# Gated cross-attention and a gated expert layer on one core: root refinements, normalised tiles and small constants moved to GpSimd, output accumulators begun from turned x_mid, new orders

## What is computed

```python
x = x + tanh(g_xattn[0]) * xattn(ctx_768, layernorm(x), mask, ...)
#   xn = layernorm(ctx)*g+b; ln = layernorm(latents)*g+b       (latents = layernorm(x))
#   q = ln @ Wq.T;  k, v = split(concat([xn @ Wkv.T, ln @ Wlkv.T]))
#   attn = softmax(where(mask, rmsnorm(q)*SCALE @ rmsnorm(k).T, -max));  out = attn @ v @ Wo.T + bo
x = x + tanh(g_ffn[0]) * ffn(layernorm(x), expert_sel, keys, values)
#   gates = sigmoid(x @ expert_sel.T); the best 4 of 32 are kept, the others are 0
#   out = (relu(x @ keys) * gate) @ values                     (32 experts of 64)
```

## Time and profile before

| | us |
|---|---|
| median of 3 runs | 115.79 (115.44 to 116.35) |
| the profiled execution | 115.75 |
| its span, first to last instruction | 114.0 |
| TensorE busy | 105.8 (93%) |
| VectorE busy | 95.0 (83%) |
| ScalarE busy | 65.6 (58%) |
| GpSimd busy | 16.0 (14%) |

### The profile page before, as it was taken

How to read it: one execution, slowest core, us unless ns; L and a number is a source line. 1 busy time by engine, 2 the same in 40 slices (tenths; PEclk the granted TensorE clock), 3 DMA queues, 4 the chain that set the end, 5 groups by cost and what they waited for, 6 DMA issues and landing times.

```text
span 114.0 us, 2086 instructions
## 1 busy us (share of the span) xinstructions
PE 105.8 (93%) x644; PEld 86.1 (76%) x644; DVE 95.0 (83%) x309; ACT 65.6 (58%) x148; POOL 16.0 (14%) x26
## 2 busy tenths in 40 slices
PE   4993998999999999999989999999999999999980
PEld 4983987868668597959879766678888888888860
DVE  5776688968789699688597999997999999889982
ACT  4918999999879958084611322470666455444410
POOL 6021000002100869140000400000420000000000
PEclk9999999999999999999999999999999999999999
DMA  3789800000000000000001987586008987532004
GB/s 86 223 179 397 376 10 3 3 6 0 0 0 0 6 0 0 0 3 6 0 12 49 297 270 255 178 255 198 3 12 285 299 244 229 214 126 83 0 30 154
DMA packets 7112, 12.78 MB, mean 112 GB/s; under 512 B 894, under 2 KB 2558, under 8 KB 6847
## 3 DMA queue, kind: packets, MB, share of 16 engines
q1 hardware_dynamic: 7102, 12.67, 34.3%
HBM read 12.00 MB, written 0.66 MB: 111 GB/s over the span
## 4 chain that ended last, share of the span: by engine, by line
PE 74%; ACT 12%; DMA 4%; DVE 3%; SPq 3%; issue 1%; DVEq 1%
PE bank L724 13%; PE bank L726 13%; PE bank L725 13%; PE bank L862 10%; PE bank L849 5%; DMA bo<-wb_in 4%; PE bank L916 3%; PE bank L754 3%; PE bank L783 3%; PE bank L794 2%; PE bank L820 2%; PE bank L847 2%; ACT cx L594 1%; ACT kT L657 1%; PE bank L887 1%
## 5 line engine op out<-in xcount | busy, mean ns | idle before, releaser
L701 ACT ACTIVATE hid_hi<-keys 128x512 fp32r<-128x512 f32 x28 | 17.4, 632 | 16.8 <-DVE keys L535 13.1
L535 DVE SCALAR_TENSOR_TENSOR keys<-bank,inT 128x512 f32<-128x512 f32 x32 | 21.2, 686 | 1.1 <-PE bank L726 0.8
L552 DVE TENSOR_TENSOR hid_lo<-keys,hid_hi 128x512 fp32r<-128x512 f32 x28 | 18.4, 686 | 0.1
L862 PE MATMUL bank<-vw,prob 128*128 128x129 f32 x128 | 15.7, 278 | 0.2 <-ACT prob L670 0.2
L862 PEld LDWEIGHTS bank<-vw,prob 128*128 128x128 f32 x128 | 14.8, 191 | 1.0 <-issue 1.0
L724 PE MATMUL bank<-xm_hi,k_lo 128*128 128x512 f32 x32 | 13.7, 427 | 0.0
L726 PE MATMUL bank<-xm_hi,k_hi 128*128 128x512 f32 x32 | 12.5, 391 | 0.0
L725 PE MATMUL bank<-xm_lo,k_hi 128*128 128x512 f32 x32 | 12.5, 390 | 0.0
L445 DVE CUSTOM_DVE_ANT_0 junk<-bank,mask_b 128x512 bf16<-128x512 f32 x16 | 10.4, 689 | 2.0 <-PE bank L820 1.8
L724 PE MATMUL bank<-hid_hi,v_lo 128*128 128x512 f32 x28 | 11.3, 402 | 0.0
L670 ACT ACTIVATE prob<-bank 128x512 f32<-128x512 f32 x16 | 8.7, 594 | 4.0 <-PE bank L849 3.8
(11 more groups left out here) (131 smaller groups left out, 198.8 us busy)
## 6 DMA issues: line engine op xcount, KB each, us to landing
inT<-gate_rows SPq DMA_DIRECT2D x32, 256.0 KB, 3.6
keys<-keys_in SPq DMA_DIRECT2D x1, 1024.0 KB, 7.5
values<-values_in SPq DMA_DIRECT2D x1, 1024.0 KB, 9.5
out<-x_mid SPq DMA_DIRECT2D x4, 128.0 KB, 1.8
vecs_x<-x_in SPq DMA_DIRECT2D x1, 256.0 KB, 5.0
wa<-wa_in SPq DMA_DIRECT2D x1, 208.0 KB, 2.9
cx<-ctx_in SPq DMA_DIRECT2D x2, 96.0 KB, 2.6
cx<-ctx_in SPq DMA_DIRECT2D x1, 192.0 KB, 5.5
```

Source lines behind the costliest of these rows:

```text
L535: dve.scalar_tensor_tensor(hid[:, n % 3, :], bank[H_BANK[n % len(H_BANK)]][:, :], 0.0, gated[:, n % SLOTS, :], ALU.max, ALU.mult).then_inc ...
L552: dve.tensor_tensor(hid_lo[:, m % RING, :], hid[:, n % 3, :], hid_hi[:, m % RING, :].bitcast(F32), ALU.subtract).then_inc(hid_lo_ready, 1)
L701: act.activation(hid_hi[:, m % RING, :], hid[:, n % 3, :], ACT.Copy).then_inc(hid_hi_ready, 1)
L862: last = pe.matmul(bank_of(b, OUT + t)[:, WOA * a:WOA * a + WOA], prob[:, b % 2, a, j, P * t:P * t + P], vw[:, b, j, a, :], start=(j == 0) ...
```

## The change

GpSimd gets an order of its own and takes over stages:

- `norm_in` (root refinement, nb, the x tiles), `newton_qk` (the refinement of `norm_qk`; VectorE's `norm_qk` then waits for `rs_qk_ready`), `norm_mid` whole, the rounded parts of expert_sel (`split_sel`), 1 + exp for the sigmoid (`add_one`) and the scaling of bo (`scale_bo`, before at the end of ScalarE's `constants`). The refinement is four instructions there, each waiting for the one before. GpSimd's wait for `max_done` ahead of the low parts is gone, and each quarter is a stage.
- `turn_res` writes x_mid transposed into the accumulator bank as its first contents; every `down` adds to it. The gates are scaled by tanh(g_ffn) when they are copied out, and `finish` is a plain copy: for the first half on ScalarE, for the second on VectorE. `x_midT` and ScalarE's copy of it are gone.
- The orders of TensorE, VectorE and ScalarE are new.

```diff
 PE_ORDER = """
...
+    warm 13, warm 14, turn_in 0, warm 15, warm 16, warm 17, warm 18, fold 0, project 0, turn_in 1, vlat 0,
+    vctx 0, warm 19, project 1, vlat 1, warm 20, turn_qk 0, turn_in 2, warm 21, vctx 1, warm 22, warm 23,
+    row_max 0.0, vlat 2, vctx 2, row_max 0.1, turn_in 3, turn_qk 1, project 2, turn_max 0, vlat 3, row_max 1.0,
+    weights 0.0, vctx 3, row_max 1.1, weights 0.1, project 3, turn_max 1, turn_qk 2, attend 0.0, weights 1.0,
+    row_max 2.0, turn_qk 3, weights 1.1, row_max 2.1, row_max 3.0, attend 0.1, turn_max 2, attend 1.0,
+    row_max 3.1, attend 1.1, weights 2.0, turn_max 3, turn_mid 0, weights 2.1, weights 3.0, select 0, turn_mid 1,
+    attend 2.0, select 1, weights 3.1, turn_gates 0, attend 2.1, turn_gates 1, attend 3.0, attend 3.1,
+    turn_res 0, turn_mid 2, up 0.0, up 0.1, select 2, up 0.2, turn_res 1, up 0.3, up 0.4, down 0.0, down 0.1,
+    turn_mid 3, down 0.2, up 0.5, down 0.3, up 0.6, up 0.7, up 0.8, down 0.4, up 0.9, up 0.10, down 0.5,
+    down 0.6, select 3, turn_gates 2, up 0.11, down 0.7, down 0.8, up 0.12, turn_gates 3, up 0.13, up 0.14,
+    turn_res 2, down 0.9, turn_res 3, down 0.10, up 0.15, up 1.0, down 0.11, down 0.12, up 1.1, down 0.13,
...
+POOL_ORDER = """
+    norm_in 0, norm_in 1, scale_bo 0, add_bias 0, newton_qk 0, norm_in 2, mask 0, norm_in 3, newton_qk 1,
+    low_values 0, newton_qk 2, newton_qk 3, low_values 1, low_keys 0, low_keys 1, add_bias 1, low_keys 2,
+    norm_mid 0, split_sel 0, low_values 2, norm_mid 1, low_keys 3, add_one 0, add_one 1, norm_mid 2,
+    low_values 3, norm_mid 3, add_one 2, add_one 3
 """
 DVE_ORDER = """
...
+    stats_in 0, stats_in 1, scale_wo 0, stats_in 2, sum_qk 0, stats_in 3, norm_qk 0, scale_gq 0, sum_qk 1,
+    row_max 0.0, norm_qk 1, row_max 0.1, turn_max 0, row_max 1.0, sum_qk 2, row_max 1.1, norm_qk 2, sum_qk 3,
+    turn_max 1, norm_qk 3, row_max 2.0, row_max 2.1, row_max 3.0, out_proj 0, turn_max 2, stats_mid 0,
+    row_max 3.1, out_proj 1, stats_mid 1, turn_max 3, turn_mid 0, turn_mid 1, select 0, select 1, out_proj 2,
+    stats_mid 2, out_proj 3, turn_mid 2, stats_mid 3, up 0.0, up 0.1, up 0.2, select 2, up 0.3, up 0.4,
...
 ACT_ORDER = """
...
+    stats_in 0, constants 0, norm_in 0, stats_in 1, turn_in 0, norm_in 1, fold 0, project 0, turn_in 1,
+    stats_in 2, sum_qk 0, vlat 0, vctx 0, project 1, stats_in 3, norm_in 2, turn_qk 0, round_qk 0, turn_in 2,
+    sum_qk 1, vlat 1, norm_in 3, vctx 1, vlat 2, vctx 2, turn_in 3, turn_qk 1, round_qk 1, split_values 0,
+    project 2, weights 0.0, vlat 3, sum_qk 2, vctx 3, weights 0.1, project 3, turn_qk 2, sum_qk 3, round_qk 2,
+    split_values 1, weights 1.0, turn_qk 3, round_qk 3, weights 1.1, split_keys 0, split_keys 1, split_values 2,
+    split_keys 2, split_values 3, stats_mid 0, split_keys 3, weights 2.0, turn_mid 0, stats_mid 1, weights 2.1,
...
+            def newton(y, v, w):
+
+                then(pool.tensor_tensor(w[:, 1, :], y, y, ALU.mult))
+                then(pool.tensor_tensor(w[:, 2, :], w[:, 1, :], v, ALU.mult))
+                then(pool.tensor_scalar(w[:, 1, :], w[:, 2, :], -0.5, 1.5, ALU.mult, ALU.add))
+                return pool.tensor_tensor(w[:, 3, :], w[:, 1, :], y, ALU.mult)
...
+            def norm_in(b):
+                pool.wait_ge(var_ready, b + 1)
+                pool.tensor_scalar(nm_in[:, b, :], mv_in[:, b, BT:, 0], -1.0, None, ALU.mult)
+                pool.wait_ge(y0_in, b + 1)
+                then(newton(rs_in[:, b, 0, :], var_in[:, b, :], rs_in[:, b, :, :]))
+                pool.tensor_tensor(nb_in[:, b, :], nm_in[:, b, :], rs_in[:, b, 3, BT:], ALU.mult).then_inc(nb_ready, 1)
+                for t in range(BT):
+                    j = BT * b + t
+                    pool.tensor_scalar(xn[:, j, :], x[:, j, :], mv_in[:, b, t, 0:1],
+                                       rs_in[:, b, 3, t:t + 1], ALU.subtract, ALU.mult).then_inc(xn_ready, 1)
...
+            def newton_qk(b):
+                pool.wait_ge(ms_ready, b + 1)
+                pool.wait_ge(y0_qk, b + 1)
+                newton(rs_qk[:, b, 0, :], ms[:, b, :], rs_qk[:, b, :, :]).then_inc(rs_qk_ready, 1)
...
+            def norm_mid(b):
+                pool.wait_ge(var_mid_ready, BT * (b + 1))
+                pool.tensor_scalar(var_mid[:, b, :], mv_mid[:, b, :, 1], LN_EPS, None, ALU.add)
+                pool.wait_ge(y0_mid, b + 1)
+                then(newton(rs_mid[:, b, 0, :], var_mid[:, b, :], rs_mid[:, b, :, :]))
...
             def norm_qk(b):
-                dve.wait_ge(ms_ready, b + 1)
-                dve.wait_ge(y0_qk, b + 1)
-                newton(rs_qk[:, b, 0, :], ms[:, b, :], rs_qk[:, b, :, :])
+                dve.wait_ge(rs_qk_ready, b + 1)
...
-                dve.wait_ge(exp_ready, b + 1)
-                then(dve.tensor_scalar(one_e[:, t, :], exp_l[:, t, :], 1.0, None, ALU.add))
+                dve.wait_ge(one_ready, b + 1)
...
             def finish(h):
+                dve.wait_ge(down_done, EC * (h + 1))
                 for b in range(HB * h, HB * h + HB):
...
+                    dve.tensor_copy(res[:, b, :], acc(b)).then_inc(res_ready, 1)
...
-                act.wait_ge(in_bo, 16)
-                act.activation(bo[:, :], bo[:, :], ACT.Copy, scale=tanh_g[:, 0:1]).then_inc(bo_ready, 1)
...
-                act.activation(gateT[:, b, :], bank_of(b, TURN_GATES)[0:E, 0:S], ACT.Copy).then_inc(gateT_ready, 1)
+                act.activation(gateT[:, b, :], bank_of(b, TURN_GATES)[0:E, 0:S], ACT.Copy,
+                               scale=tanh_g[0:E, 1:2]).then_inc(gateT_ready, 1)
...
-                                     start=(c == 0), stop=(c == EC - 1))
+                                     start=False, stop=(c == EC - 1))
...
             def turn_res(b):
                 pe.wait_ge(mid_ready, BT * (b + 1))
...
+                pe.wait_ge(gateT_ready, HB * (b // HB + 1))
+                for t in range(BT):
+                    pe.matmul(acc(b)[:, P * t:P * t + P], x_mid[:, BT * b + t, :], ident[:, :],
+                              start=(b % HB == 0 and t == 0), stop=False, is_transpose=True)
```

More of the change, by code:

```diff
@@ L57 @@
     warm 0, warm 1, warm 2, warm 3, warm 4, warm 5, warm 6, warm 7, warm 8, warm 9, warm 10, warm 11, warm 12,
-    warm 13, warm 14, warm 15, warm 16, warm 17, warm 18, turn_in 0, warm 19, warm 20, project 0, turn_in 1,
-    fold 0, project 1, vctx 0, vlat 0, turn_in 2, vlat 1, warm 21, warm 22, turn_qk 0, vctx 1, warm 23, vlat 2,
-    turn_qk 1, row_max 0.0, vctx 2, turn_in 3, row_max 0.1, row_max 1.0, vlat 3, project 2, turn_max 0, vctx 3,
-    weights 0.0, project 3, weights 0.1, row_max 1.1, turn_qk 2, attend 0.0, turn_max 1, row_max 2.0, turn_qk 3,
@@ L86 @@
+    split 1.8, up 1.10, up 1.11, split 1.9, split 1.10, up 1.12, up 1.13, split 1.11, split 1.12, up 1.14,
+    up 1.15, split 1.13, split 1.14, split 1.15, finish 1
 """
 ACT_ORDER = """
-    stats_in 0, constants 0, stats_in 1, norm_in 0, turn_in 0, norm_in 1, project 0, turn_in 1, stats_in 2,
-    fold 0, project 1, norm_in 2, sum_qk 0, vctx 0, vlat 0, turn_in 2, sum_qk 1, vlat 1, turn_qk 0, stats_in 3,
-    vctx 1, round_qk 0, turn_qk 1, norm_in 3, round_qk 1, turn_in 3, vlat 2, vctx 2, split_keys 0, project 2,
@@ L91 @@
-    vlat 3, vctx 3, sum_qk 2, weights 0.0, project 3, weights 0.1, sum_qk 3, turn_qk 2, round_qk 2, split_keys 1,
-    split_values 0, turn_qk 3, round_qk 3, weights 1.0, split_keys 2, split_keys 3, weights 1.1, weights 2.0,
-    stats_mid 0, turn_mid 0, split_values 1, weights 2.1, stats_mid 1, weights 3.0, select 0, turn_mid 1,
-    weights 3.1, select 1, turn_gates 0, turn_gates 1, stats_mid 2, turn_mid 2, split_values 2, select 2,
-    stats_mid 3, split 0.4, split 0.5, split 0.6, split 0.7, turn_mid 3, turn_res 0, split 0.8, turn_gates 2,
@@ L100 @@
+    turn_mid 2, stats_mid 3, select 2, turn_mid 3, split 0.4, split 0.5, split 0.6, split 0.7, split 0.8,
+    turn_gates 2, select 3, split 0.9, split 0.10, turn_gates 3, split 0.11, split 0.12, split 0.13, split 0.14,
+    split 0.15, split 1.0, split 1.1, split 1.2, split 1.3, split 1.4, finish 0, split 1.5, split 1.6, split 1.7,
+    split 1.8, split 1.9, split 1.10, split 1.11, split 1.12, split 1.13, split 1.14, split 1.15
 """
```

170 lines of the change are left out of this document (68 added, 102 removed).

## The result

The changed kernel takes 118.75 us (median; 118.72 to 120.37), the kernel before in the same comparison 116.07: ratio 1.027, 95% interval 1.017 to 1.037. The forecast was 113.5 us, range 111.8 to 116.3, with a chance of 0.14 for slower. The profiled execution took 120.37 us (span 118.6), and 1.6 us of that belong to it alone: the granted clock of TensorE was 0.51 from 54.4 to 57.8 us (the lower of its two levels, 1.2 GHz; 2.4 before and behind), after TensorE had been busy for only 0.33 us between 53.0 and 54.0, waiting for mid tiles. `attend 2.0` took 3.54 us there, where its like took 1.95 a little later. So some 3.0 us are to be explained, against a span of 114.0.

The account below looks back on a forecast made before the run. TensorE bounds the kernel behind 10.07 us, with its large idle piece at the start; -2.4 - 0.5 + 0.3 + 0.4 + 0.6 - 0.3 - 0.2 - 0.1 = -2.2 us gave 113.5 us, range 111.8 to 116.3.

Parts of the forecast that it names:

- the price of a tile: Normalised 128x128 tile on GpSimd: taken as 0.3 us, a pair 0.6, as on VectorE.
- the forecast's +0.6: Third mid normalisation (norm_mid 2): 4.9 us on GpSimd against 4.1, a loss of 0.6 us (0 to 1.0).
- The refinement was over-priced: Root refinement on GpSimd: four steps at 0.35 us, 1.4 us against 0.6 on VectorE, +0.8 (+0.2 to +1.2).
- Rival B: GpSimd's small steps at 0.45 us expose chains and eat the gain: about 116 us, or 115 half exposed; chance 0.19.
- Part 1: Start: ScalarE freed from bo, GpSimd refines early; cx normalised 2.6 us sooner, -2.4 us carried out of the start.
- rival E: Start: loads of batch 2 and wb set the time anyway, -1.2 in place of -2.4: 114.7 us; chance 0.10.
- Part 2: 10 to 45 us: GpSimd's later refinements covered, VectorE relieved of some 13 us; TensorE's idle time shrinks, -0.5 us.
- Part 3: Mid norms 0, 1 and 2 late by +0.3, +0.4, +0.6 us; turn_gates 1 no longer waits, -0.3.
- rival C: Before 60 us: GpSimd's queue becomes the bound, refinements behind low parts; slower, 119.5 us at worst; chance 0.13.
- Part 4: Expert stage -0.2 us (turn_res into accumulators, ScalarE's copy dropped); end -0.1 us (copy instead of multiply-add).
- long out: Expert stage: turn_res needs its half's gates out of the same bank; taken as already out.
- Rival D: GpSimd and VectorE lock each other, mainly in the expert stage: 113.5 to 114.5 us; chance 0.58 together with forecast.

Follow-up runs that it names:

- the probe: Kernel before plus eleven unused GpSimd instructions at the start: 128x128 tile 0.30 us with two constants, 0.86 to 0.94 with two SBUF scalars; no kernel time given.
- the start alone: Kernel before with bo scaled on GpSimd, batch 0 normalised ahead of batch 1's statistics, mask behind the fourth normalised tile: 115.45 us, ratio 0.998.
- The mid part alone: Kernel before, its orders kept, with norm_mid (refinement and tiles) on GpSimd and GpSimd's wait for max_done gone: 118.50 us, ratio 1.027.
- the unused tile: Kernel before with one unused tile of 32 bytes a partition added behind ln_mid: 116.65 us, ratio 1.007.
- GpSimd's queue mended: Changed kernel with another POOL_ORDER only: second bias earlier, third low parts of keys and values behind norm_mid 0 and 1: 117.71 us, ratio 1.017.
- the front alone: Kernel before with norm_in, newton_qk and bo scaling on GpSimd, norm_in 0 ahead of stats_in 1 on ScalarE: 117.25 us, ratio 1.016.
- the accumulators: Kernel before with only the accumulators begun from turned x_mid, gates scaled when copied out, finish a copy: 116.33 us, ratio 1.006.

## Why the prediction was wrong

**The step that failed first is the price of a tile**: "A normalised 128x128 tile: between 0.20 [...] and 0.32 [...]; I take 0.3, a pair 0.6, as on VectorE". It is 0.80, a pair 1.59, measured in the changed kernel's trace for all sixteen tiles. Both bounds came from instructions without a scalar operand from SBUF (a memset, a subtraction of two tiles); the probe shows that this operand is what costs. The upper bound did not contain the value, so neither did the range of any sum built on it. The pair costs 1.0 us more in each of eight chains, and the second tile comes 0.78 us behind the first, which TensorE feels as a wait of its own. No run shows what this term alone is worth in the kernel's time, since the runs with the tiles back on VectorE met the lock. The third mid pair, with no low part in front, gives an estimate: the forecast's +0.6, 1.0 more for the pair and 0.3 less for the refinement make 1.3 us; the wait was 1.38. The scaling of bo, one scalar from SBUF on 128x128, took 0.61 us where 0.2 to 0.3 was forecast, for the same reason.

**The refinement was over-priced**: steps 0.285 us apart against 0.35, a refinement 1.1 us against 1.4 (and 0.6 on VectorE). GpSimd's timeline at the start:

```profile
5.02 0.20 POOL L354 TENSOR_TENSOR rs_in<-rs_in 128x4 f32<-128x4 f32 x1 [0.22 <-ACT rs_in L605]
5.30 0.20 POOL L355 TENSOR_TENSOR rs_in<-rs_in,var_in 128x4 f32<-128x4 f32 x1
...
6.33 1.59 POOL L371 TENSOR_SCALAR xn<-vecs_x,mv_in,rs_in 128x128 f32<-128x128 f32 x2
```

Rival B was built on slow steps and had the wrong cause.

**Part 1, -2.6 at the transposes, -2.4 carried.** ScalarE took up cx at 6.38 us (forecast 6.65). TensorE transposed cx at 8.24, not 7.4, because its x transposes wait for the pair of tiles: -1.8. At `attend 0.0` 0.45 us were left (33.97 against 34.42): the waits of 1.07 us at 18.23 and 0.53 at 24.33 (0.30 and 0.45 before, at 11.24 and 18.08), and four more warm-up matmuls behind the first transposes, account for most of the rest. That is less than rival E left (-1.2), and by another cause. That the sum treats a gain at the start as a gain at the end is right in the old orders only while no lock turns over: with the start alone it passed through attention whole, and half of it was lost at 80 us.

**Part 2, -0.5** came out as a loss, inside the figures just given. VectorE's busy time fell by 11.2 us (13 forecast), but its row maxima waited 5.8 us for TensorE in all, against 2.0 before: the freed time was worth nothing.

**Part 3, +0.3, +0.4, +0.6, -0.3: this is the loss.** TensorE's waits at the three mid normalisations are 0.92, 1.02 and 1.38 us, 3.3 us in all and nearly none before: without the 1.6 us of the clock, the first expert matmul comes 3.5 us late, having been 0.45 ahead at `attend 0.0`. Low parts stand in front of the first two, as rival C had it; C's place was right, its price was put on the steps and its chance (0.13) was too low. The gain at `turn_gates 1` came (no wait there), too small to matter. The mid part alone in the old orders delays the last matmul by 3.0 us: 0.9 by the first two pairs (`turn_gates 1` at 59.39 against 58.50), 1.5 by the third, and 0.6 in the expert stage, where the unused tile of the same size alone costs 0.8; so these are the placing of tiles and not GpSimd's work.

**Part 4, -0.2 and -0.1**: by themselves +0.6% in the old orders. In the trace the expert stage is 1.3 us longer, 0.65 of it the wait for the turned gates, which the forecast took for "long out". In the new orders no such wait shows; there the expert stage is 0.4 us shorter than the earlier trace rows has it, 0.22 of it because one turned pair now stands ahead of it.

**Rival D** was right that the lock goes both ways, and wrong that it matters little before 62 us: it priced VectorE's steps with two inputs only, and the normalised tiles are held as well. In the changed kernel itself it cost nothing that the trace shows (its 128x512 groups on VectorE keep their 682 to 686 ns); it decided the kernels made from it.

**What adds up to 3.0 us** is read from the changed kernel's trace: 0.45 ahead at `attend 0.0`, 3.3 us of waits for GpSimd's mid tiles and 0.6 of smaller pieces behind it, 0.4 back in the expert stage. The experiments support it in part: the mid part alone costs 3.0 us in the old orders, 2.4 of them ahead of the expert stage; GpSimd's queue mended gives back 1.0. They are not a sum: the front alone costs 1.8 (0.8 of it the placing), the accumulators 0.7, in old orders. How much of the loss is the tile's price and how much the queue, and whether the new orders cost anything, stays open.

## What to carry to other kernels

Before an operation moves to another engine, find a row there of the same form, with the same kind of scalar operand, and not only of the same size; if there is none, the upper bound has to be several times the nearest row. A staged engine that works strictly in order is judged by what stands in its queue when a late result arrives, not by its busy share: 36% busy, and 21% of the critical chain. Where GpSimd and VectorE both read SBUF, look which of them starts first at each meeting, since a shift of 0.3 us between them turns the outcome over. When a stage is moved back to see what it cost, look in the trace whether its instructions take their usual time, since an experiment can run into such a meeting too. And compare kernels with the same SBUF layout, or measure the layout by itself.
